# Moving eight products per sample from GpSimd to VectorE, with new instruction orders on all engines, in a two-layer transformer kernel

## The reference, cut to what matters

```
x = x + ga * attention(norm(x))                # block 0: 16 heads of width 8, relative positions, softmax
x = x + gb * experts(norm(x))                  # block 0: 16 experts, the best 4 weighted by softmax
x = x + ga * memory(norm(x))                   # block 1: running sums over the tokens of v times rotors
x = x + gb * mix(norm(x))                      # block 1: token-shift feed-forward with sigmoid and squared relu

experts:  gate = min(x Wg + bg, 7);  up = clip(x Wu + bu, -7, 7)
          act  = (up + 1) * gate * sigmoid(1.702 gate)
          out  = sum over e of score[t, e] * (act_e Wd_e + bd_e)      # score is 0 for 12 of 16 experts
```

## Time and profile before

| | |
|---|---|
| median of three runs | 1395.64 us |
| profiled execution, span from first to last instruction | 1390.0 us |
| lies around the span (median less span) | 5.6 us |
| from start to the end of sample 0's experts | 106 us |
| one steady step (15 equal intervals between 106.1 and 1325.2 us) | 81.27 us |
| from the end of sample 15's experts to the end | 64.8 us |

### The profile page before, as it was taken

The page is one execution under the profiler, slowest core; times in us unless marked ns, Lnnn a source line. Parts: engine busy times, 40 slices in busy tenths (PEclk is TensorE's granted clock), DMA queues, the critical chain, the costliest instruction groups (busy, mean ns, idle before and its releaser), DMA issues.

```text
span 1390.0 us, 22686 instructions
## 1 busy us (share of the span) xinstructions
PE 1248.1 (90%) x7130; PEld 938.9 (68%) x7130; DVE 1136.3 (82%) x2104; ACT 970.5 (70%) x1699; POOL 280.8 (20%) x258
## 2 busy tenths in 40 slices
PE   7798998989899898989989898998989899898989
PEld 5475775758577575757758575775857577585778
DVE  7758879797987979798797979879797987979765
ACT  1665767778676777867677786767778676776841
POOL 4030221303022130302213031221303122130200
PEclk9899999999999999999999999999999999999999
DMA  5330301204030110403012030301204030120000
GB/s 126 93 35 5 35 9 16 20 8 34 8 34 8 15 19 8 34 8 32 10 13 21 8 34 8 31 10 13 21 8 34 8 31 11 12 22 5 1 4 4
DMA packets 54392, 29.82 MB, mean 21 GB/s; under 512 B 3725, under 2 KB 53338, under 8 KB 54362
## 3 DMA queue, kind: packets, MB, share of 16 engines
q1 hardware_dynamic: 52472, 28.74, 17.2%
q10 hardware_dynamic: 1890, 0.70, 0.5%
HBM read 8.20 MB, written 2.10 MB: 7 GB/s over the span
## 4 chain that ended last, share of the span: by engine, by line
PE 56%; DVE 14%; ACT 14%; issue 10%; POOL 2%; DMA 1%; SPq 1%; ACTq 1%; DVEq 0%; POOLq 0%
PE ring L762 15%; PE pb L862 7%; PE pa L776 7%; DVE smax L1814 5%; PE pa L680 4%; PE ring L667 3%; PE ring L716 3%; PE pb_k L792 2%; DVE prod L1927 2%; ACT prob L1279 2%; PE ring L749 2%; PE ring L629 2%; PE pb_v L820 1%; ACT L1383 1%; ACT frac L1386 1%
## 5 line engine op out<-in xcount | busy, mean ns | idle before, releaser
L427 POOL TENSOR_TENSOR gsc<-gsc,sc_all 128x512 f32<-128x512 f32 x128 | 175.7, 1377 | 353.2 <-ACT gsc L1344 353.2
L762 PE MATMUL ring<-ht,wgu 128*128 128x256 f32 x1024 | 241.5, 384 | 1.0 <-ACT sc_all L1332 1.0
L1954 DVE TENSOR_TENSOR_SCAN prod<-keep,prod 128x512 f32<-128x512 f32 x188 | 224.2, 1214 | 0.0
L762 PEld LDWEIGHTS ring<-ht,wgu 128*128 128x128 f32 x1024 | 193.2, 191 | 34.8 <-issue 5.0
L1814 DVE TENSOR_REDUCE smax<-ring 128x4 f32<-128x1024 f32 x128 | 153.3, 1219 | 17.6 <-PE ring L629 10.8
L1887 DVE SCALAR_TENSOR_TENSOR prob<-prob,gsc 128x512 f32<-128x512 f32 x120 | 81.4, 688 | 81.9 <-POOL gsc L427 63.5
L862 PE MATMUL pb<-prod,wo 128*128 128x256 f32 x544 | 129.3, 382 | 5.9 <-DVE prod L1968 5.8
L1279 ACT ACTIVATE prob<-ring 128x1024 f32<-128x1024 f32 x128 | 125.7, 1024 | 5.1 <-PE ring L667 3.5
L1339 ACT ACTIVATE gsc<-ring,gub_t 128x256 f32<-128x256 f32 x256 | 110.5, 501 | 21.3 <-PE ring L762 21.0
L776 PE MATMUL pa<-prob,wdown 128*128 128x256 f32 x512 | 122.0, 380 | 1.8 <-DVE prob L1881 1.8
L862 PEld LDWEIGHTS pb<-prod,wo 128*128 128x128 f32 x544 | 102.0, 190 | 25.2 <-DVE prod L1968 12.0
(11 more groups left out here) (284 smaller groups left out, 2476.1 us busy)
## 6 DMA issues: line engine op xcount, KB each, us to landing
q_rows<-qk_part SPq DMA_DIRECT2D x144, 64.0 KB
k_rows<-qk_part SPq DMA_DIRECT2D x135, 64.0 KB
x_in<-in_L_attn_x_dram SPq DMA_DIRECT2D x16, 128.0 KB, 2.1
sc_all<-_L_ffn_gate_up_proj_dram SPq DMA_DIRECT2D x1, 2048.0 KB, 11.9
out_dram<-xo SPq DMA_DIRECT2D x16, 128.0 KB, 1.8
prob<-in_L_wmod_dram SPq DMA_DIRECT2D x2, 384.0 KB, 3.9
k_rows<-qk_part ACTq DMA_DIRECT2D x9, 64.0 KB
wo<-in_L_attn_Wo_dram SPq DMA_DIRECT2D x1, 512.0 KB, 7.4
```

The lines of the kernel that those rows point to most:

```text
L427: pool.tensor_tensor(gsc[:, n % NG, :], gsc[:, n % NG, :], sca, ALU.mult).then_inc(S["gsc"], 1)
L762: last = mm(ring[:, n % 2, g * 512 + j * L:g * 512 + (j + 1) * L], lhsT=wgu[:, 2 * n + j, g, :], rhs=ht[:, :], start=True, stop=True, skip ...
L1954: nc.vector.tensor_tensor_scan(prod[:, h, n - 1, :], keep[:, :], prod[:, h, n - 1, :], 0.0, ALU.mult, ALU.add).then_inc(S["cu" + str(n)], 1)
```

## The change

1. `expert_pair(a, 0..7)` leaves the step of POOL. A new VectorE function `expert_mul` does the same product on the same tile, one call per pair, in the step of VectorE. `first`, that is sample 0, keeps `expert_pair` on POOL.
2. The step boundary moves: `scores(nx, 7)`, `phases` 0 and 1, `phase_values` 0 and 1, `time_values(0)`, `turn_max` and `phase(0)` stand at the end of the step before.
3. The lists of the steady step on TensorE, ScalarE and VectorE get a new order, as do `first` and `last`.
4. `warm_last` is gone; in `last`, `mix_3` stands before the last four warm matmuls. Some waits move from the lists into the functions (`is_first`), with no effect on the order.

```diff
             def step(a, b, nx):            # GpSimd
...
-                if on_a:
-                    expert_pair(a, 0)
-                    expert_pair(a, 1)
...
-                    expert_pair(a, 6)
                 if on_b:
                     deviation(b, "4", vepsb, rstdb)
                 if on_a:
-                    expert_pair(a, 7)
                     deviation(a, "3", vepsb, rstdb)
...
+            def expert_mul(b, n):          # VectorE
+                need(dve, "silu", b, n + 1)
+                need(dve, "bc", b, n // 2 + 1)
+                sca = sc_all[:, 2 * n:2 * n + 2, :].rearrange("p e t -> p (e t)")
+                tt(gsc[:, n % NG, :], gsc[:, n % NG, :], sca, ALU.mult).then_inc(S["gsc"], 1)
...
-            def warm_last(nx, n):
-                if nx is None:
-                    warm(n, ring[:, 0, :])
```

More of the change, by code:

```diff
@@ L960, in step @@
                     memory_wo(b, 0)
-                if on_x:
-                    head_3(nx)
                 if on_a:
                     mean(a, "2", x1[:, :], "x1", pa, ())
-                if on_x:
-                    head_5(nx)
+                if on_b:
+                    phases(b, 3)
                 if on_a:
@@ L976, in step @@
                     router(a)
+                if on_x:
+                    head_5(nx)
+                if on_b:
+                    sums_1(b, 2)
+                    memory_wo(b, 1)
+                if on_a:
+                    warm_scores(a, 2)
+                    turn_scores(a)
+                if on_x:
+                    head_6(nx)
+                if on_a:
+                    broadcast(a, 0)
+                    broadcast(a, 1)
                 if on_b:
@@ L1015, in step @@
                 if on_a:
-                    down_pair(a, 3)
                     down_pair(a, 4)
+                if on_x:
+                    scores(nx, 0)
                 if on_b:
                     variance(b, "4", pb, sqb)
-                if on_a and on_x:
-                    scores(nx, 0)
+                if on_a:
+                    down_pair(a, 5)
+                if on_x:
                     scores(nx, 1)
@@ L1528, in step @@
                     mix_2(b)
+                if on_a:
+                    phase(a, 0)
             def first(a, nx):
@@ L1557, in first @@
                 copy_broadcast(a, 2)
+                part_2(nx)
                 copy_broadcast(a, 3)
-                part(nx)
-                part_2(nx)
                 gate_clip(a, 0)
@@ L2035, in step @@
                 if on_b:
+                    memory_a(b, 1)
+                    memory_b(b, 0)
                     memory_p(b, 0)
+                    memory_c(b, 0, 3)
+                    memory_p(b, 1)
+                    memory_o(b, 0, 2)
+                    memory_c(b, 0, 4)
+                    memory_o(b, 0, 1)
+                    memory_c(b, 1, 2)
+                    memory_b(b, 1)
                 if on_x:
```

451 lines of the change are left out of this document (214 added, 237 removed).

## The result

| | kernel before | changed kernel |
|---|---|---|
| median of 20 runs | 1396.05 us | 1388.3 us |
| lowest to highest | 1393.47 to 1399.94 | 1380.77 to 1405.18 |
| profiled execution, its span | 1390.0 us | 1392.0 us (time 1393.73) |

What follows compares the result with a forecast made beforehand. No single engine bounds the kernel; PE is nearest, busy 73.8 of 81.3 us a step. 14 x - 1.55 = - 21.7, - 3.1 last step, - 3 `first`, - 0.7 `last`: - 28.5 us, 1367 us, range 1350 to 1397.

Steps and rivals of the forecast that it cites:

- the likeliest case: Whole kernel: the case of the sum, steps of 79.7 us and 1367 us, 1355 to 1382 by itself; chance 0.49.
- a step above 81: Steady step: a sign that the prediction is wrong, where the sum had a step of 79.7 us.
- the walk up to the split: Steady step: first three stretches 10.15, 10.75 and 10.5 us; split of q and k ready 14.0 us after `router`.
- VectorE's 73.8: VectorE in a steady step: busy 68.7 + 5.5 - 1.1 = 73.1 us, range 72 to 74.
- The 0.25 for a drop of the clock at the end: Last step without warm matmuls: rival, clock drops, + 3 us, at most + 6; chance 0.25, on top of any case.
- the transfers take 22.4 us, the new wait is 1.5 us: Before `scores(nx,0)`: transfers land 22.4 us after the split, TensorE waits 1.5 us at L629, stretch 36.45 us.
- TensorE's own work "34.9": From `router`: TensorE's own work would let `scores(nx,0)` start 34.9 us later; the transfers allow 36.4.
- the wait of 1.26 at 107.30 goes: In `first`: `part_2` starts some 2.8 us earlier, so TensorE's 1.26 us wait for a transfer goes.
- - 3 us in `first`: In `first`: wait of 1.26 us and half-clock time behind it go, - 3 us together, between - 1 and - 5.
- the transfers don't bind: Stretch from `router` to `scores(nx,0)`: rival, 34.9 us, a step of 78.2, - 50 us, 1346 us; chance 0.15.
- The products: Steady step: moving eight products from GpSimd to VectorE alone brings nothing, a step of 81.4 us.
- The table loads: ScalarE, L1383 and L1317: both loads go, 2.57 us a step; the stretch to `router` gains 1.9 us.

Runs made afterwards that it cites:

- By part: Changed kernel with the 18 transfers of q and k issued in three groups of six, each as soon as its part is ready: 1352.77 us, 0.9682.
- half rows: Changed kernel with each of the 18 transfers of a steady step carrying only half of its rows: 1353.27 us, 0.970.
- the split earlier: Changed kernel with ScalarE's part(nx) ahead of tables(b, 3) and part_2(nx) ahead of copy_broadcast(a, 0) in the steady step: 1378.0 us, 0.9875.
- the edit of the transfers: Kernel before with the 18 transfers issued in three groups, each as its part of the split is ready, nothing else: 1391.59 us, 0.9958.
- the fastest version: Transfers in three groups on the changed kernel, plus TensorE's down_bias moved from ahead of broadcast(3) to behind gate_up(1): 1344.25 us, 0.963.

## Why the prediction was wrong

The forecast of 28.5 us less was some four times what was measured. The range held the time, the likeliest case did not, and the cause is no rival on the list: the mechanism chosen for the sum happened, at a higher price than the sum had. The step that failed is the landing of the transfers, put at 22.4 us behind the split and measured at 24.4; beside it, TensorE's clock in a steady step had no term at all. Of the prediction's signs of being wrong, a step above 81 came true (81.21 in the mean).

- **Right: the walk up to the split.** The first three stretches came within 0.16 us each, the split of q and k within 0.25, the four table loads a step are two (33 where 63 were, and two at the start), VectorE's 73.8 us and GpSimd's 6.87 a step lie in the ranges given. The last step (77.17) and `last` (62.04 for 64.8) did better than the sum by 1.0 and 2.1 us. The 0.25 for a drop of the clock at the end did not come true: the row of 1329.96 to 1392.00 has a granted clock of 1.00, with the warm matmuls gone. So the drop that the prediction took as to be expected from the Trainium skill (TensorE: Matmul & The Clock Gate, What's actually happening) is not seen in this run. By part has one there, at 1296 to 1298.
- **In part luck: VectorE's 73.8.** Eight products add 4.9 us and not 5.5, an estimate from the 3.8 of the old order with the 1.1 of `memory_d` added back. And the 1.1 counted as won is lost again elsewhere, by 1.9 us a step: GpSimd's split now holds up two scans in each step (last section).
- **Wrong: the term "the transfers take 22.4 us, the new wait is 1.5 us".** It measured 24.4 in the mean, 22.1 to 27.1; TensorE's weight loads, which stand first, waited 2.1 us a step in the mean and 5.2 at most, and one wait in sample 0, where none was forecast, was 4.4 at the matmuls. The 22.3 of the earlier trace rows was the end of the traffic, not the release of who waits for it: the two lie 2.0 us apart at 923.4 and 925.40 (the row below has traffic for 0.4 of its microsecond) and 2.3 at 593.7 and 595.93. The Trainium skill (DMA: Bandwidth & Descriptors, Anatomy of one DMA) puts most of a fixed cost of about 2 us behind the last byte, in the receipt ahead of the semaphore; it describes another kind of queue; these two places agree. The check against the earlier trace rows seemed to confirm 22.4, but there, by the trace of before, traffic ends at about 106.4 (DMA share 0.66 in the microsecond to 106, 0.29 in the next) and TensorE starts at 107.30, 0.9 later, which does not agree with the Trainium skill. Two places that agreed were two different sums.

```profile
923.00:924.00 1.00, 1.00 (x6) 0.87 (x6) 0.68 (x2) 0.98 (x4) 0.00 (x0) 1.00 0.26 17
```

- **Wrong: TensorE's own work "34.9".** By part, where nothing is waited for, `scores(nx, 0)` starts 35.9 us after `router` in a step without a fall of the clock. The landing hid this term in the changed kernel.
- **Wrong: no term for the clock in a steady step.** The prediction named a fallen clock for the ends alone and read a granted clock of 1.00 off the step before. There, TensorE was not idle for more than 1.0 us at a time. The changed kernel makes it wait up to 4.8 us just ahead of the experts' end, and in the rows above the clock goes to 0.50 at such a wait. Its busy time is 13.0 us above that of two runs in which the transfers land in time (1243.6 against 1230.6, half rows and by part). The third such run, the split earlier, has 1241.5; in it TensorE waits longer elsewhere (19.9 us for `vt`). So a share of the loss goes with this wait; which waits bring a fall is open. The Trainium skill (TensorE: Matmul & The Clock Gate, What's actually happening) has the throttled state as the default that activity releases; the prediction cited this for the last sample and had the earlier trace rows in hand, and did not ask it of its own new wait.
- **Wrong: "the wait of 1.26 at 107.30 goes" and - 3 us in `first`.** The split was ready at 83.48 instead of 84.75, but the release came at the same 107.28: landing is not a constant behind the split. And `scores(nx, 0)` now stood ahead of `down_pair` 6 and 7, so that `x2` waited too: 111.77 against 106.08, + 5.7. The change has that order in `first` too, and the prediction priced only the split.

The sum again with what was measured: 14 steady steps and the last took 1218.2 us where the forecast had 14 x 79.7 + 78.2 = 1194.0, + 24.2. The first `x2` came 8.7 us after the forecast, and the end was 2.1 us shorter than forecast. Together + 30.8, against 30.5 between the spans (1392.0 and 1361.5).

By stretch, us, the mean of the 14 steps that have transfers, from one `phases(0)` to the next:

| stretch | before | forecast | changed | by part |
|---|---|---|---|---|
| to the first exponential | 11.01 | 10.15 | 10.20 | 10.34 |
| to the end of `copy_values` | 10.67 | 10.75 | 10.59 | 10.50 |
| to `router` | 12.46 | 10.5 | 10.60 | 10.60 |
| to `scores(nx,0)` | 35.26 | 36.45 | 38.14 | 36.17 |
| to `phases(0)` | 11.82 | 11.85 | 11.92 | 11.53 |

The fourth stretch alone is 14 x (38.14 - 36.45) = 23.7 of the + 24.2. In the last one two misses cancel, which is luck: it takes 11.1 to 11.5 us in nine steps and 12.8 to 14.0 in the five in which the clock falls at the scores, some 11 us in all for these falls.

By part has no such wait, and its span is 40.2 us shorter than the changed kernel's: 8.4 ahead of the first `x2`, 32.75 in the steps, and 0.94 lost in the end. The steps' part is about the 24.1 us of waits at L621, all of them behind the first `x2`, and 9.1 of the 13.0 us of busy time (of the rest, 5.5 lie ahead of the first `x2`, and by part has 1.6 more behind the last). The prediction's rival "the transfers don't bind" had a step of 78.2 and 1346 us; with the wait taken away it is 78.8 to 79.2 and 1352.8.

**The products** were called worth nothing alone. In the old order they cost 25 us, with `expert_mul` where I put it. In the new order without the transfers' wait they are worth 41 us, and the new order without them is worth 2.7 (1394.1 against 1396.8). In these placements neither half is the gain; both are needed:

| | products on GpSimd | on VectorE |
|---|---|---|
| old order | 1396 | 1422 |
| new order, transfers as changed | 1404 | 1388 |
| new order, transfers by part | 1394 | 1353 |

The last column also shows that the change did most of what it could and then lost it at one place. **The table loads** were put at 2.57 us of ScalarE and a gain of 1.9 in the stretch to `router`; put back into the run by part they cost 2.1 a step, of which 1.3 stand in steps without a fall of the clock. And 878.34 - 877.05 = 1.29 is the load alone: the drain that the Trainium skill (ScalarE: Activation LUTs, What ACT_TABLE_LOAD costs) adds to it, which the prediction weighed, is not seen here either.

**Open.** Why the transfers of one step take 22 us and those of another 27: the last issues of the queue are slower in the long ones (1.25 to 1.35 us each at 579 to 583, where the step at 902 to 914 has 0.61 up to its last two, 1.01 and 1.12), but what slows them was not tried. Why the clock falls behind a wait of 0.94 us in one step and not in the next. Where the edit of the transfers wins 5 us in the kernel before. And what else of the new order does what: only three places of it were taken apart.

## What to carry to other kernels

A semaphore that a DMA raises comes later than the end of its traffic, here by 0.9 to 2.3 us. And the same 18 transfers landed 22.1 to 27.1 us behind the split in one run. So a transfer that was hidden by 11 us gives no landing time that a new order may lean on within some 5 us; leave that margin, or issue each piece as soon as it is ready. When a change puts a new wait in front of TensorE, price it twice: once for the wait, and once, as a case with a chance (5 of 13 here), for the matmuls behind it at the 1.2 GHz level. And an edit that costs 25 us in one order can win 41 in another, so price order and placement together.

## What the runs showed of the hardware

The clock fell in steady steps that are 90% busy, behind waits of 0.94 to 4.8 us; in the profiled execution of the kernel before it did not fall behind the first scores. The loss differs from run to run, and the time with it: the 20 runs of the changed kernel have mean granted clocks of 0.966 to 0.980 and span 24 us, the slower ones mostly at the lower clock (correlation - 0.8); those by part have 0.984 to 0.987 and span 3.

`memory_d` is no longer held up by GpSimd; the scans are. (In the kernel before, all 15 calls of the line in the earlier trace rows that took over 1.7 us overlap a product of GpSimd.) Single lines of the changed kernel, ns minimum/median/maximum:

```profile
L1944 DVE TENSOR_TENSOR_SCAN prod<-keep,prod x188: 1191/1216/2180, 127.6 to 1370.8; 128x512 f32<-128x512 f32 x188
```

```profile
L413 POOL TENSOR_TENSOR rstdh<-vepsh,mhalf x16: 699/1528/1532, 5.6 to 1196.5; 128x2 f32<-128x2 f32 x16
```

A scan of 1.2 us takes up to 2.18, and a power of 128x2 that GpSimd does in 0.70 takes 1.53: at 873.50 it starts while VectorE is in its scans. All 28 scans above 1.4 us, two in each of 14 steps, overlap a product of GpSimd's split of q and k; in the kernel before none of the 188 is above 1.23. One of the two stands just ahead of `vt`, for which TensorE waits 0.94 us at `down_bias`:

```profile
563.36 1.31 POOL L419 TENSOR_TENSOR qk<-qk,qk_part 128x512 f32<-128x512 f32 x1 [10.34 <-ACT qk_part L1244]
...
563.58 2.18 DVE L1944 TENSOR_TENSOR_SCAN prod<-keep,prod 128x512 f32<-128x512 f32 x1
...
566.26 0.47 DVE L1793 TENSOR_TENSOR vt<-pa,vbias 128x128 f32<-128x128 f32 x2
```

The scan is 0.96 us longer than its median there, as much as the wait. So the wait that the fastest version takes out by its order may come from this overlap; no run tests that. With the products gone from GpSimd, VectorE and GpSimd still hold each other up where the few that are left meet a scan.
